# One more wait before each group of gathers in a four-layer graph network

## The reference

```python
x = _layernorm(x + _L0_gnn_ref(x, edge_index, ...))                 # attention, 4 heads of 32
x = _layernorm(x + _L1_gnn_ref(x, edge_index, edge_attr_32, ...))   # two-layer network per edge
x = _layernorm(x + _L2_gnn_ref(x, ..., src, dst, edge_type_8))      # 8 relations, gated
x = _layernorm(x + _L3_gnn_ref(x, edge_index, ...))                 # attention, 4 heads of 32
```

## Time and profile before

| what | value |
| --- | --- |
| median of 3 runs | 4506.77 us (4503.96 to 4507.35) |
| profiled execution, span from first to last instruction | 5314.6 us |
| GpSimd busy in the span | 3165.2 us (60%) |
| TensorE busy, mean granted clock | 3112.7 us (59%), 0.674 of full |
| VectorE busy | 2515.0 us (47%) |
| ScalarE busy | 1308.4 us (25%) |

### The profile page before, as it was taken

One profiled execution on the slowest core, in us unless ns is written; L12 is line 12 of the kernel. 1 busy time (PEld: TensorE's weight loads), 2 busy tenths in 40 slices (PEclk: granted clock), 3 DMA queues, 4 the chain that ended last, 5 costly groups with the idle time before them and its releaser, 6 DMA issues. The chain is left out here.

```text
span 5314.6 us, 52198 instructions
## 1 busy us (share of the span) xinstructions
PE 3112.7 (59%) x15416; PEld 2793.1 (53%) x15416; DVE 2515.0 (47%) x5316; ACT 1308.4 (25%) x3470; POOL 3165.2 (60%) x3335
## 2 busy tenths in 40 slices
PE   2666666666377787777871323333332666666666
PEld 2665666566366676666731223323231666666665
DVE  2344444445377878777870111112121454554555
ACT  0010010011267777777760000000000011111111
POOL 5666666663566666666206666666654666666662
PEclk6556556666689888988895566665665565555656
DMA  5444444443444444444241111111112333333331
GB/s 140 128 144 139 151 142 140 151 140 110 138 134 145 147 144 144 143 144 148 81 189 47 48 49 49 50 49 47 52 43 67 97 95 97 99 95 97 98 96 52
DMA packets 284107, 567.22 MB, mean 107 GB/s; under 512 B 108648, under 2 KB 157034, under 8 KB 283802
## 3 DMA queue, kind: packets, MB, share of 16 engines
q0 software_dynamic: 119664, 280.17, 20.3%
q1 hardware_dynamic: 157082, 278.92, 15.4%
q10 hardware_dynamic: 7056, 4.56, 0.3%
HBM read 465.83 MB, written 97.56 MB: 106 GB/s over the span
## 5 line engine op out<-in xcount | busy, mean ns | idle before, releaser
L840 POOL DMA_INDIRECT rows<-gat_table,src_i x1662 | 1568.6, 944 | 861.4 <-issue 464.9
L1593 POOL DMA_INDIRECT rows<-mlp_table,src_i x831 | 789.5, 950 | 527.0 <-issue 303.8
L1254 POOL DMA_INDIRECT rows<-rel_table,rel_i x831 | 783.9, 943 | 494.8 <-issue 343.4
L1129 PE MATMUL p_sum<-rows,hot 128*128 128x133 f32 x3328 | 781.6, 425 | 14.2 <-DVE rows L906 12.5
L1121 PEld LDWEIGHTS p_adc<-adw,hot_t 128*128 128x128 f32 x3328 | 688.1, 314 | 178.0 <-DVE hot_t L880 127.5
L1121 PE MATMUL p_adc<-adw,hot_t 128*128 128x8 f32 x3328 | 678.0, 342 | 147.7 <-DVE hot_t L880 108.4
L1129 PEld LDWEIGHTS p_sum<-rows,hot 128*128 128x128 f32 x3328 | 735.9, 326 | 17.2 <-DVE rows L906 15.6
L1411 PE MATMUL p_sum<-hot,rows 128*128 128x128 f32 x1664 | 324.5, 363 | 715.9 <-DVE hot L1281 365.9
L1411 PEld LDWEIGHTS p_sum<-hot,rows 128*128 128x128 f32 x1664 | 298.6, 272 | 744.3 <-DVE hot L1281 381.2
L1061 ACT COPY sums<-p_sum 128x133 f32<-128x133 f32 x208 | 56.4, 271 | 2211.6 <-DMA rel_index<-rel_i 1902.6
L1889 PE MATMUL p_sum<-hot,rows 128*128 128x128 f32 x3328 | 476.0, 310 | 201.8 <-ACT rows L1799 107.7
(11 more groups left out here) (239 smaller groups left out, 3693.9 us busy)
## 6 DMA issues: line engine op xcount, KB each, us to landing
drow<-in_dst_rows SPq DMA_DIRECT2D x208, 512.0 KB
hot_table<-hot SPq DMA_DIRECT2D x104, 512.0 KB
hot<-hot_table SPq DMA_DIRECT2D x104, 512.0 KB
rows<-gat_table,src_i POOLq DMA_INDIRECT x1662
rel_table<-rows SPq DMA_DIRECT2D x49, 512.0 KB, 2.6
eat<-in_edge_t SPq DMA_DIRECT2D x104, 128.0 KB
rows<-mlp_table,src_i POOLq DMA_INDIRECT x831
rows<-rel_table,rel_i POOLq DMA_INDIRECT x831
```

Source lines behind the costliest of these rows:

```text
L840: pool.indirect_dma_start(out=rows[:, n % RING, t, :], out_offset=None, in_=net.gat_table[:, :], in_offset=bass.IndirectOffsetOnAxis(ap=ne ...
L1129: end = nc.tensor.matmul(p_sum[:, 0:SUMS], hot[:, n % HALF, t, :], rows[:, n % RING, t, 0:SUMS], start=(t == 0), stop=(t == T - 1))
L1254: pool.indirect_dma_start(out=rows[:, n % RING, t, :], out_offset=None, in_=net.rel_table[:, :], in_offset=bass.IndirectOffsetOnAxis(ap=ne ...
L1593: pool.indirect_dma_start(out=rows[:, n % RING, t, :], out_offset=None, in_=net.mlp_table[:, :], in_offset=bass.IndirectOffsetOnAxis(ap=ne ...
```

## The change

In all three `gather` functions, which serve the four passes, GpSimd waits before the gathers of group n until all rows of group n - 1 are in SBUF. The first group of a pass has no such wait.

```diff
             def gather(n):
                 wait(pool, s.summed, n - RING + 1)
+                if n:
+                    pool.wait_ge(s.gathered[(n - 1) % RING], landed(sh, n - 1))
                 for t in given(sh, n):
                     pool.indirect_dma_start(
                         out=rows[:, n % RING, t, :], out_offset=None, in_=net.gat_table[:, :],
...
             def gather(n):
                 wait(pool, s.summed, n - RING + 1)
+                if n:
+                    pool.wait_ge(s.gathered[(n - 1) % RING], landed(sh, n - 1))
                 for t in given(sh, n):
                     pool.indirect_dma_start(
                         out=rows[:, n % RING, t, :], out_offset=None, in_=net.rel_table[:, :],
...
             def gather(n):
                 wait(pool, s.summed, n - RING + 1)
+                if n:
+                    pool.wait_ge(s.gathered[(n - 1) % RING], landed(sh, n - 1))
                 for t in given(sh, n):
                     pool.indirect_dma_start(
                         out=rows[:, n % RING, t, :], out_offset=None, in_=net.mlp_table[:, :],
```

## The result

The median after the change is 5470.8 us (5467.7 to 5474.2), against 4505.7 us (4504.0 to 4507.4) for the kernel before on the same chip: a ratio of 1.214 [1.2125, 1.2155], 965 us more, 2.34 us for each of the 412 new waits. The forecast was 628 us more, so the direction held and the size did not: the time lies above the range of 4880 to 5300 us.

A forecast was written before the change was run, and what follows sets the result against it. The prediction took the timed run as bound by GpSimd issuing gathers back to back. Added waits, 103 x 1.45 + 309 x 1.55 = 628 us on 4506.8, gave 5135 us (bounds 4985 to 5429); the stated range was 4880 to 5300 us.

The forecast's parts named there:

- The reading of the timed run out of a profile that didn't match it: Timed run, all four passes: GpSimd issues gathers back to back, 4155.8 us; at most 74 us of stops left.
- The wait was not hidden: Rival at the borders: full-ring stops of 674 us cover the new wait, 0 to 50 us added; 9%.
- the rows did not land sooner in a timed run: Rival at the borders: tracing stretches the landing, so untraced 1.085 us is added per border, 4954 us; 12%.
- nothing got faster: Rival in the gat passes: a shorter queue frees SyncE's loads waiting behind gathers, about 4433 us; 2%.
- The estimate from the Trainium skill: Gather landing by the skill's page: 2.15 to 2.3 us, 0.9 to 1.05 us added per border, 4897 us in all.
- the stop is between 1.64 us (GpSimd as quick as TensorE) and 1.87 us: Relation pass borders: landing plus GpSimd's restart, 1.34 to 1.57 us added, 1.45 us taken.
- I choose 1.55 us, near the quiet pass, since even there about half of the DMA time is free: Gat and mlp passes: added time per border, near the relation pass's; 309 borders make 479 us.
- The upper bound of the sum, 5429 us: Whole kernel: 103 borders at 1.57 us and 309 at 2.46 us, 922 us added.
- The 2.46 us allowed for the busy passes: Gat and mlp borders, upper bound: landing grows to 2.54 us as the DMA engines' free share shrinks.
- The 1.57 us of the relation pass: Relation pass borders: upper bound of the added time, a 1.87 us stop less the 0.305 us gap.
- The span foretold for the profile, 5330 to 5550 us: Profiled execution after: stops exist already at 5314.6 us, so it grows far less than the timed runs.
- a slower TensorE: Profiled execution before: TensorE runs slower there than in timed runs, for a cause its rows don't name.

The follow-up runs named there:

- e8_before_again: The kernel before, profiled once more with no edit; 4504.5 us.
- e3_two_back: Against the changed kernel, the wait is for the landing of the group two before instead of the group before; 4506.2 us, ratio 0.9998.
- e7_fifth_gather: Against the changed kernel, the landing wait stands ahead of a group's fifth gather instead of its first; 4507.3 us, ratio 1.0003.
- e1_swap: Against the changed kernel, the two waits before a group are swapped in the source, landing first, ring second; 5337.1 us, ratio 1.1841.
- e5_load_moved: On top of e1_swap, SyncE's 512 KB load in the gat passes also waits for logits, so it comes early in a group of gathers; 5175.9 us, ratio 1.1486.
- e6_rel_only: Against the kernel before, the change's two added lines stand in the relation pass alone; 4717.8 us, ratio 1.047.
- e4_second_gather: Against the changed kernel, the landing wait stands ahead of a group's second gather instead of its first; 5052.1 us, ratio 1.1211.

## Why the direction was right and the size wrong

**What held.** The reading of the timed run out of a profile that didn't match it was right: e8_before_again has 0.305 us between its gathers and no ring stops to speak of. So did the mechanism: every border pays a landing and a restart, GpSimd sets the pace, nothing hides it and nothing is paid back (964.5 of 964.8 us are GpSimd's idle time). A gather still takes 0.95 us. TensorE starts on the rows 1.64 us after the issue, as read from the earlier trace rows, and where the gather carries the landing wait alone, GpSimd follows 0.15 us later, within the 0 to 0.23 that was taken. e3_two_back and e7_fifth_gather show the other side: the same wait on rows that have had 5 us or more to land is free.

The rivals fell. The wait was not hidden, the rows did not land sooner in a timed run, and nothing got faster. The estimate from the Trainium skill ("DMA: Bandwidth & Descriptors", "Anatomy of one DMA") had 2.15 us for a gather of the relation pass, whose rows are the shortest, and ended at 0.9 to 1.05 us a border. The runs are above it: the landing there took 2.5 us (median) in the kernel after, and even the cleanest borders, of the relation pass in e1_swap, add 188.7 / 103 - 0.305 = 1.53 us.

**What failed** is the sum, by 965 - 628 = 337 us. Two of its terms were too small: GpSimd's restart behind a landing, taken as 0 to 0.23 us later than TensorE's, and the landing in the gat passes, which the 1.55 us took to be nearly that of the quiet pass. By pass:

| pass | predicted, us | after | e1_swap | e5_load_moved |
| --- | --- | --- | --- | --- |
| relation, 103 borders | 149 | 212.6 | 157.3 | 156.3 |
| mlp, 103 | 160 | 246.3 | 187.4 | 184.5 |
| gat, 206 | 319 | 505.6 | 495.9 | 326.2 |

(Growth of GpSimd's idle time before gathers against e8_before_again. The busy time of the gathers was 12 us lower in e1_swap and e5_load_moved than in after and e8_before_again, so their spans grew by that much less. The profiled execution of e5_load_moved was 18.5 us shorter than its median, so its gat figure may be low by up to that.)

1. The restart failed first: "the stop is between 1.64 us (GpSimd as quick as TensorE) and 1.87 us". It took the new wait as part of the gather that it releases; "no instruction is added but the wait itself" was priced at nothing. From the ninth group of a pass the landing wait is an instruction of its own ahead of the gather, and GpSimd starts 0.68 us after TensorE instead of 0.15. Undone in e1_swap, this gave back 55 us in the relation pass and 59 in the mlp pass. That the source's order of two waits decides it was not in the prediction at all.
2. A part of these 114 us is a second gap that nothing foretold: at the second gather of every eighth group GpSimd's gap is 1.11 us instead of 0.305, twelve times a pass, 48 x 0.805 = 39 us in the whole kernel. It is there in the kernel after, in e6_rel_only and, on top of the stop at that gather, in e4_second_gather, and in none of the other runs. In the gat passes it makes 19 us.
3. The step "I choose 1.55 us, near the quiet pass, since even there about half of the DMA time is free" failed in the gat passes, with 505.6 us against 319. Once the load is moved and the waits are in the other order, the gat passes cost 326.2 us, that is 1.58 a border: the number chosen is near to what a landing costs there when the load doesn't meet it. The other 179 us are the collision with SyncE's load, the separate instruction and 19 us of the gap in point 2. They can't be split further, since in e1_swap the shorter border moved the load and the landing closer together: at the borders shown, the load is issued 323.93 - 322.31 = 1.62 us ahead of the group's last gather in the kernel after (rows at the end of this document) and 1.12 us in e1_swap. So it seems that the collision ate what the order had saved. The average share of the DMA engines, from which the prediction reasoned, says nothing of this: the load follows the group's landing through the consumers, so it comes at one place of the group's period, and that place was the end.
4. The mlp pass is under-sized by 187.4 - 160 = 27 us on its own, 1.82 us a border for 1.55. Its rows are twice as long as those of the relation pass, and its gathers land after 2.8 us against 2.5; that the length is the cause is argued, not shown. The rival, SyncE's loads of that pass, has little for it: at about nine of ten borders in e1_swap they are issued 3.4 us or more ahead of the last gather. The relation pass was 8 us off (1.53 for 1.45), within the bounds given.

Points 1, 2 and 4 make 55 + 59 + 27 + 8 = 149 us, point 3 makes 186, together 335 of 337; the rest is rounding.

The upper bound of the sum, 5429 us, missed too, and the range stopped at 5300, with some 5% of the chance put above it. The 2.46 us allowed for the busy passes held (505.6 / 206 = 2.45 and 246.3 / 103 = 2.39), but by luck: they were worked out for a slower landing alone, while 59 of the mlp pass's 246.3 us came from points 1 and 2. The 1.57 us of the relation pass, which was thought to be known, was exceeded by half a microsecond, through the same two points.

The span foretold for the profile, 5330 to 5550 us, came true (5467.5), but for a wrong reason: it was worked out for an execution stretched like that of the earlier trace rows, and this one is not. Rows from the first gat pass of the stretched execution show where it lost time; behind them stand the same rows of e8_before_again:

```profile
307.62 3.89 PE L1129 MATMUL p_sum<-rows,hot 128*128 128x133 f32 x16
...
315.23 0.27 ACT L1061 COPY sums<-p_sum 128x133 f32<-128x133 f32 x1 [10.71 <-DMA rel_index<-rel_i]
```

```profile
309.61 3.56 PE L1129 MATMUL p_sum<-rows,hot 128*128 128x133 f32 x16
...
313.21 0.27 ACT L1061 COPY sums<-p_sum 128x133 f32<-128x133 f32 x1 [9.47 <-PE p_sum L1129]
```

In the first execution ScalarE goes on 3.72 us after the end of TensorE's add-up as the profile has it, in the second 0.04 us after it; the add-up itself takes 3.89 and 3.56 us. So "a slower TensorE", as the prediction concluded, isn't what these rows show: the end of its work reached the others late, and GpSimd found the ring full. What caused that stays open; no other execution here shows it.

## What to carry to other kernels

On the engine that sets the pace, a wait for a transfer that this engine has just issued costs the landing and a restart each time (a stop of 1.8 us here, 2.3 to 2.7 with what came on top), although the ring behind it holds eight groups; the same wait four gathers later, or on the group before last, is free. If two waits stand ahead of one instruction, let the one that is satisfied last be the instruction's own (here by putting it first in the source), and count what a new wait lines up in time: transfers on other queues that follow the same event can meet it at every turn. Where a profile's span is not the timed run's, profile once more before reading stops from it.

## What was not expected of the hardware

- A separate wait instruction ahead of a gather delays it only if it is the wait that releases it: GpSimd starts 0.68 us after TensorE on the same rows instead of 0.15. Satisfied early, 384 of them cost nothing (e3_two_back, 0.9998).
- A 512 KB load that is issued among the last gathers of a group delays their landing: the gat stop is 2.71 us on average with it and 1.89 without, 3.13 against 1.83 at the borders shown, though the DMA engines are busy for less than half of the first gat pass (share 0.46 in the kernel after). What in the engines delays it was not tried.
- The gap at the second gather of every eighth group, which is every 64th gather, is 1.11 us long. Here it is in the first gat pass of the kernel after, behind the load and the last gather of the group before. Its cause stays open:

```profile
322.31 0.33 SPq L789 DMA_DIRECT2D drow<-in_dst_rows  x1
...
323.93 0.94 POOL L842 DMA_INDIRECT rows<-gat_table,src_i  x1 [0.30 <-issue]
327.28 0.94 POOL L842 DMA_INDIRECT rows<-gat_table,src_i  x1 [2.41 <-DMA rows<-gat_table,src_i]
...
329.34 0.94 POOL L842 DMA_INDIRECT rows<-gat_table,src_i  x1 [1.11 <-issue]
```
